# A 400 byte fill behind every second row gather in place of a 280 byte fill behind each one

## The chip, the cores and the metric

The kernel runs on one core of one Trainium2 chip. The metric is the device time of one execution in microseconds; the median of the runs shown counts.

## The reference, cut to what matters

The program is one layer of a graph network with attention, and behind it a mixture of experts. Only the first concerns the change, since it is there that rows are gathered.

```python
def _L0_gnn_ref(inputs, conv_weights, attn_l, attn_r, h_bias, edge_src, edge_dst, edge_type):
    # 3750 nodes, 123750 edges, 8 relations, 4 heads of 64
    feat_all = jnp.einsum('ni,rhid->rnhd', inputs, conv_weights)
    feat_src_e = feat_all[edge_type, edge_src]
    feat_dst_e = feat_all[edge_type, edge_dst]
    el = jnp.sum(feat_src_e * attn_l[edge_type], axis=-1)
    er = jnp.sum(feat_dst_e * attn_r[edge_type], axis=-1)
    e = jax.nn.leaky_relu(el + er, negative_slope=LEAKY_SLOPE)
    m = jax.ops.segment_max(e, edge_dst, num_segments=N_NODES)
    ex = jnp.exp(e - m[edge_dst])
    denom = jax.ops.segment_sum(ex, edge_dst, num_segments=N_NODES)
    alpha = ex / denom[edge_dst]
    h = jax.ops.segment_sum(alpha[..., None] * feat_src_e, edge_dst, num_segments=N_NODES)
    return h.reshape(N_NODES, OUT_FEAT) + h_bias
...
x = x + gnn(layernorm(x))
x = x + ffn(layernorm(x))      # 8 experts, 256 -> 512 -> 256, gelu, the two best of 8 by a gate
```

## The kernel before, in words

**First part** (to about 286 us). TensorE computes every node's features for every relation and ScalarE's queue writes them to `table` in HBM, one row of 264 floats for each node and relation. Beside it VectorE counts the edges of each node and ranks the nodes by degree; GpSimd gathers lists (`dchunk`, L337), scatters the nodes in their new order (`ranked`, L344) and gathers the first 64 indices of each node's edges (`idx_all`, L351, with a fill of its own behind each, L354, which the change leaves as it is).

**Second part.** The nodes are taken in W = 30 windows of 128, one node to a partition. For window w GpSimd issues one gather for each slot k: the instruction fetches, for each of the 128 nodes, the table row of its k-th incoming edge, into `rows[par][:, k, :]`. `par` is w mod 2, so there are two buffers of NS = 40 slots. The first SURE = 20 gathers of a window are always there; those after are issued one by one as long as the window's largest degree is over k (`more`). Edges past 40 come in batches of 8 into `xrows`, from L967 and L969 through the same helper (`gather`, L899) and without fills.

Behind each row gather stands a fill: `spaced_gather` (L922 to L925) issues the gather and then a memset of 280 bytes in each partition of a tile `spacer`, which nothing ever reads. The memsets at k = 9 and k = 19, and the one byte memset `space_end` at the end of a window, raise the semaphore `spaced`; GpSimd itself waits for it before it writes the same piece of `spacer` again.

**Order on GpSimd.** Between k = 7 and k = 8 of window w it issues the scatter of window w - 3's output (`scatter`, L907), which waits until VectorE has finished that output (L1228). At k = 0, 8, 16 and 24 it waits for `freed`: window w - 2 has folded that part of the buffer. The gathers of window w + 1 are issued while window w is worked on.

**The other engines.** When the rows of window w have landed (SyncE relays the last semaphore, L850), VectorE forms the attention scores (`prepare`, with L1023 the first instruction that needs the rows), ScalarE and VectorE weigh the rows (L1388, L1061), VectorE sums them (L1065), normalises the result and turns it into `z`; TensorE runs the experts of window w - 1 (L1485, L1499) and VectorE adds them up (L1222). In the first windows VectorE also works through the `xrows` batches (L1135 to L1142). After the last window its experts run alone.

Of the kernel before, what the change touches and what calls it, by code (L numbers as in the profile page):

```python
# [26 lines left out]
U8 = mybir.dt.uint8  # L27
AX_X = mybir.AxisListType.X

P = 128  # L30
# [69 lines left out]
def build(nc, x, src, dst, etype, conv, attn_l, attn_r, h_bias, gate_w, gate_b, W1, b1, W2, b2, out):  # L100
# [29 lines left out]
    with ctx:  # L130
        def sb(name, shape, dt=F32, stack=ctx):
            return stack.enter_context(nc.sbuf_tensor(name, shape, dt))


        ident = sb("ident", [P, P])
        idx_all = sb("idx_all", [P, W, CHUNK], U32)
        typ_all = sb("typ_all", [P, W, CHUNK], BF16)
        rank_sb = sb("rank_sb", [P, W, 4], I32)
        nb_row = sb("nb_row", [1, 2 * W], I32)
        slot_id = sb("slot_id", [P, CHUNK])  # L140
        wa = sb("wa", [P, KD, 2 * R * H])

        phase1(nc, sb, sem, locals())
        phase2(nc, sb, sem, locals())
# [483 lines left out]
def phase2(nc, sb, sem, env):  # L628
# [10 lines left out]
    SURE = 20  # L639
# [26 lines left out]
    oid = [sb(f"oid{i}", [P, 1], U32) for i in range(2)]  # L666
    typ_cur = [sb(f"typ_cur{i}", [P, CHUNK]) for i in range(2)]
    hot9 = sb("hot9", [P, NS, R1])
    PAUSE = 280
    spacer = sb("spacer", [P, SURE, PAUSE], U8)  # L670
    space_end = sb("space_end", [P, 1], U8)
    er_hot = sb("er_hot", [P, NS, H, R1])
    score = sb("score", [P, NS, H])
# [91 lines left out]
    def after(eng, s, value):  # L765

        if not isinstance(value, int) or value > 0:
            eng.wait_ge(s, value)

    def windows(eng, window):  # L770

        for w in range(2):
            window(w, w, 0)
        with eng.Fori(1, W // 2) as j:
            for par in range(2):
                window(j * 2 + par, par, j)
# [4 lines left out]
    def next_window(eng, act_on, w, par, half):  # L781

        if isinstance(w, int) or par == 0:
            act_on(w + 1, 1 - par, half + par)
        else:
            with eng.If(w < W - 1):
                act_on(within(w + 1), 1 - par, half + par)

    def alone(eng, passed):

        eng.sem_inc(passed, 1)
# [16 lines left out]
    def further_batches(eng, nb, batch, chunk):  # L808


        def chain(s, c, left):
            if s == SLOTS:
                return
            with eng.If(left > s):
                batch(s, c * SLOTS + s if not isinstance(c, int) else s, c)
                chain(s + 1, c, left)

        chain(STATIC, 0, nb)
        with eng.If(nb > SLOTS):
            with eng.Fori(1, (nb + (SLOTS - 1)) >> 3) as c:  # L820
                chunk(c)
                chain(0, c, nb - c * SLOTS)
# [67 lines left out]
    @block.gpsimd  # L890
    def _(pool):
        q = nc.gpsimd
        bt = Batches(pool, "pool")
        chunks = pool.alloc_register("pool_chunks")
        pool.reg_mov(chunks, 0)

        def gather(buf, landed, idx, slots, col=0):
            for k in slots:
                q.indirect_dma_start(buf[:, k, :], None, table,  # L899
                                     bass.IndirectOffsetOnAxis(idx[:, col + k:col + k + 1], 0)  # L900
                                     ).then_inc(landed, 16)

        def scatter(v, par, n=P):

            pool.wait_ge(out_ok, v + 1)
            alone(pool, pool_passed)
            q.indirect_dma_start(out, bass.IndirectOffsetOnAxis(oid[par][0:n, :], 0), xo[par][0:n, :],  # L907
                                 None).then_inc(out_done[par], 16)

        def static_rows(w, par, half):  # L910

            degree = pool.value_load(nb_row[0:1, bass.ds(w * 2 + 1, 1)], min_val=0, max_val=E)  # L912
            pool.wait_ge(idx_staged, w + 1)
            alone(pool, pool_passed)

            def freed_by(s):

                if not isinstance(w, int) or w >= 2:
                    pool.wait_ge(freed, (w - 2) * PAIRED + (s + 1))
                    alone(pool, pool_passed)  # L920

            def spaced_gather(k):  # L922

                gather(rows[par], row_landed[par][min(k // SLOTS, 2)], idx_st[par], (k,))
                return q.memset(spacer[:, k % SURE, :], 0)  # L925

            after(pool, spaced, w * 3)
            for k in range(SURE):
                if k == SLOTS and (not isinstance(w, int) or w >= 3):
                    scatter(w - 3, 1 - par)  # L930
                if k % SLOTS == 0:
                    freed_by(k // SLOTS)
                last = spaced_gather(k)
                if k in (SURE // 2 - 1, SURE - 1):
                    last.then_inc(spaced, 1)
            if isinstance(w, int):
                pool.wait_ge(cleared, 1)

            def more(k):

                if k < NS:
                    with pool.If(degree > k):  # L942
                        if k == 3 * SLOTS:
                            freed_by(3)
                        if k % (SURE // 2) == 0:
                            pool.wait_ge(spaced, w * 3 + k // (SURE // 2) - 1)
                            alone(pool, pool_passed)
                        spaced_gather(k)
                        more(k + 1)

            more(SURE)
            q.memset(space_end[:], 0).then_inc(spaced, 1)

        def window(w, par, half):

            next_window(pool, static_rows, w, par, half)
            nb, g = bt.enter(w)
            degree = pool.value_load(nb_row[0:1, bass.ds(w * 2 + 1, 1)], min_val=0, max_val=E)  # L958
            pool.wait_ge(xidx_staged, w + 1)
            alone(pool, pool_passed)  # L960

            def batch(s, i, c):

                pool.wait_ge(xfolded, g + (i - STATIC + 1))
                alone(pool, pool_passed)
                idx, lo = (idx_x[par], (s - STATIC) * SLOTS) if isinstance(c, int) else (xidx, s * SLOTS)
                gather(xrows, xrow_landed, idx, range(HALF), lo)  # L967
                with pool.If(degree > i * SLOTS + HALF):
                    gather(xrows, xrow_landed, idx, range(HALF, SLOTS), lo)  # L969

            def chunk(c):
                pool.reg_add(chunks, chunks, 1)
                n = pool.snap(chunks, min_val=1)
                pool.wait_ge(xblk_ok, n)
                alone(pool, pool_passed)
                q.indirect_dma_start(xidx[:], None, edge_row.rearrange("(n o) -> n o", o=1),
                                     bass.IndirectOffsetOnAxis(xblk[:], 0)).then_inc(xblk_in, 16)
                pool.wait_ge(xblk_in, n * 16)
                alone(pool, pool_passed)

            further_batches(pool, nb, batch, chunk)
            bt.leave(w, nb, g)

        static_rows(0, 0, 0)
        windows(pool, window)
        scatter(W - 3, 1)
        scatter(W - 2, 0)
        scatter(W - 1, 1, LAST)
        for i in range(2):
            pool.wait_ge(out_done[i], 16 * (W // 2))  # L990
# [583 lines left out]
```

## Time and profile before

| | |
|---|---|
| median of 3 runs | 1950.8 us (1950.03 to 1951.86) |
| profiled execution, own time | 1945.03 us |
| its span | 1943.3 us |
| mean granted TensorE clock | 0.822 |
| busy: POOL, PE, DVE, ACT | 1458.2, 1306.2, 1299.5, 788.2 us |
| row gathers, fills behind them | 982, 982 |

The time of an execution holds the span from the first to the last instruction and a little around it, here 1.7 us. The profiled execution is one run, and it lies 5.8 us below the median of the runs that were timed. A busy share is an average over parts of the program with different limits, so the chain of waits has to tell which engine counts.

### The profile page before, as it was taken

What the parts mean: (1) busy time and instruction counts of PE and PEld (TensorE: products, weight loads), DVE (VectorE), ACT (ScalarE), POOL (GpSimd) and SP (SyncE); (2) the same over time, 40 slices, a digit from 0 to 9 for tenths busy, and PEclk for the clock granted to TensorE, in tenths of its full rate; (3) what the DMA queues carried; (4) which work ended last, traced back from release to release, by engine and by line L of the source; (5) the groups of instructions that cost most, each with busy time, mean ns of one, the idle gap of its engine ahead of it and who ended that gap; (6) DMA issues with size and microseconds to landing.
All of it is one profiled execution on the core that took longest, in us unless ns stands there. A gap on an engine that the chain in (4) does not pass through costs nothing.

```text
span 1943.3 us, 29331 instructions
## 1 busy us (share of the span) xinstructions
PE 1306.2 (67%) x6897; PEld 1044.2 (54%) x6897; DVE 1299.5 (67%) x2572; ACT 788.2 (41%) x2841; POOL 1458.2 (75%) x2199
## 2 busy tenths in 40 slices
PE   4999950027584678585858586767768585857687
PEld 1444420026474667474747475656657474746575
DVE  4633012558786888686859595968687786868782
ACT  3544420215354444353435352534444453444441
POOL 0254568868888888888888888888888888888810
PEclk9999975559787888787878888787878697877888
DMA  6366768323333233333333333333333333333300
GB/s 155 111 204 171 197 177 256 98 76 95 85 93 98 83 93 94 93 93 93 95 92 94 93 95 92 94 90 96 95 93 95 93 94 92 95 93 95 89 17 4
DMA packets 86562, 202.20 MB, mean 104 GB/s; under 512 B 32445, under 2 KB 44663, under 8 KB 82341
## 3 DMA queue, kind: packets, MB, share of 16 engines
q0 software_dynamic: 57552, 147.97, 28.2%
q10 hardware_dynamic: 9596, 33.95, 5.8%
q1 hardware_dynamic: 19201, 18.44, 3.6%
q14 instruction: 201, 1.65, 0.3%
q8 instruction: 12, 0.20, 0.0%
HBM read 160.14 MB, written 40.07 MB: 103 GB/s over the span
## 4 chain that ended last, share of the span: by engine, by line
POOL 58%; issue 16%; DVE 4%; POOLq 4%; PE 2%; ACT 1%; DMA 1%; DVEq 0%; SPq 0%; ACTq 0%
POOL rows L899 40%; POOL spacer L925 16%; POOL out_dram L907 1%; PE y_ps L1499 1%; PE hid_ps L1485 1%; POOL xrows L899 1%; POOLq L942 1%; POOLq L912 1%; POOLq L958 1%; POOLq L802 1%; DVE fold_ps L1065 1%; DVE xo L1222 0%; DMA xrows<-table,idx_x 0%; ACT rows L1388 0%; DVE rows L1061 0%
## 5 line engine op out<-in xcount | busy, mean ns | idle before, releaser
L899 POOL DMA_INDIRECT rows<-table,idx_st x982 | 947.2, 965 | 212.3 <-issue 201.1
L1499 PE MATMUL y_ps<-w,hT 128*128 128x256 f32 (+1 forms) x1920 | 518.8, 427 | 353.9 <-ACT hT L1378 353.9
L1499 PEld LDWEIGHTS y_ps<-w,hT 128*128 128x128 f32 (+1 forms) x1920 | 392.5, 211 | 443.7 <-ACT hT L1378 378.6
L1485 PE MATMUL hid_ps<-zT,w 128*128 128x128 f32 (+1 forms) x3840 | 490.3, 290 | 0.0
L1485 PEld LDWEIGHTS hid_ps<-zT,w 128*128 128x128 f32 x3840 | 479.4, 206 | 13.8 <-issue 10.8
L1388 ACT ACTIVATE rows<-rows,ex 128x65 f32<-128x65 f32 x1320 | 326.1, 347 | 115.6 <-DVE ex L1052 115.6
L1378 ACT ACTIVATE hT<-hid_ps,b1t 128x128 f32<-128x128 f32 (+1 forms) x960 | 270.5, 364 | 209.3 <-PE hid_ps L1485 209.3
L1065 DVE TENSOR_TENSOR fold_ps<-rows,fold_ps 128x780 f32<-128x780 f32 (+1 forms) x348 | 326.5, 938 | 28.4 <-DVE rows L1061 5.0
L925 POOL MEMSET spacer<- 128x280 uint8 x982 | 342.2, 348 | 0.6
L579 PE MATMUL feat_ps<-wc,xnT 128*125 128x512 f32 x480 | 220.1, 603 | 0.5 <-ACT xnT L517 0.5
L1061 DVE TENSOR_TENSOR rows<-rows,fold_ps 128x2340 f32<-128x2340 f32 (+1 forms) x76 | 189.7, 2528 | 3.9 <-DVE rows L1061 3.9
L1222 DVE SCALAR_TENSOR_TENSOR xo<-y_ps,cw,xo 128x256 f32<-128x256 f32 (+1 forms) x240 | 115.6, 482 | 39.2 <-PE y_ps L1499 33.2
L579 PEld LDWEIGHTS feat_ps<-wc,xnT 128*125 128x125 f32 x480 | 86.5, 190 | 91.1 <-issue 91.1
L1344 ACT ACTIVATE th<-e_diff 128x160 f32<-128x160 f32 x30 | 10.1, 336 | 271.0 <-DVE e_diff L1041 271.0
L1023 DVE TENSOR_TENSOR score<-score,rows 128x160 f32<-128x160 f32 x30 | 9.8, 325 | 155.9 <-SPq L850 153.2
L532 ACT COPY stage<-feat_ps 125x512 f32<-125x512 f32 x120 | 69.7, 586 | 96.0 <-PE feat_ps L579 92.2
L337 POOL DMA_INDIRECT dchunk<-in_dst_dram,chunk_u x31 | 38.4, 1237 | 90.9 <-DVE chunk_u L417 81.7
L1458 PE MATMUL zt_ps<-ident,z 128*128 128x128 f32 x60 | 14.8, 335 | 135.1 <-DVE z L1169 135.1
L907 POOL DMA_INDIRECT out_dram<-xo,oid x30 | 30.1, 1004 | 91.8 <-DVE oid L1228 87.6
L1458 PEld LDWEIGHTS zt_ps<-ident,z 128*128 128x128 f32 x60 | 7.8, 174 | 137.0 <-DVE z L1169 136.9
L1469 PE MATMUL gate_ps<-ident,xnw 128*128 128x128 f32 x60 | 12.0, 283 | 87.6 <-ACT xnw L1355 87.6
L1366 ACT COPY zT<-zt_ps 128x256 f32<-128x256 f32 x30 | 11.2, 372 | 144.7 <-PE zt_ps L1458 144.7
(197 smaller groups left out, 1142.4 us busy)
## 6 DMA issues: line engine op xcount, KB each, us to landing
table<-stage ACTq DMA_DIRECT2D x30, 924.0 KB
rows<-table,idx_st POOLq DMA_INDIRECT x982, 2.8
w<-in_L_ffn_W_dram SPq DMA_DIRECT2D x16, 512.0 KB, 13.8
node_row<-ranked SPq DMA_DIRECT2D x30, 132.0 KB, 2.3
table<-stage ACTq DMA_DIRECT2D x30, 107.2 KB
x_all<-in_x_dram SPq DMA_DIRECT2D x2, 1120.0 KB
wc<-_L_gnn_conv_weights_dram ACTq DMA_DIRECT2D x2, 1024.0 KB, 9.4
x_all<-in_x_dram SPq DMA_DIRECT2D x2, 560.0 KB
```

The costliest lines, as they stand in the source:

```text
L532: a.copy(stage[i % NSTG][:, b * RB:(b + 1) * RB, 0:AGG].rearrange("p r (h c) -> p r h c", h=H)[:, :, :, 0:HD], feat_ps[b][0:TN, :].rearran ...
L579: last = m.matmul(feat_ps[b][0:TN, :], xnT[i % NXT][:, k, :], wc[:, k, b * BANK:(b + 1) * BANK], start=(k == 0), stop=(k == KD - 1))
L899: q.indirect_dma_start(buf[:, k, :], None, table, bass.IndirectOffsetOnAxis(idx[:, col + k:col + k + 1], 0)).then_inc(landed, 16)
L907: q.indirect_dma_start(out, bass.IndirectOffsetOnAxis(oid[par][0:n, :], 0), xo[par][0:n, :], None).then_inc(out_done[par], 16)
L925: return q.memset(spacer[:, k % SURE, :], 0)
L1061: return v.tensor_tensor(o, r, bc(ex_ps[:, :, lo:hi].rearrange("p h k -> p k h"), 3, HC), ALU.mult)
L1065: return v.tensor_tensor(lanes[:, 0:n], rows[par][:, lo:lo + n, 0:AGG], lanes[:, 0:n], ALU.add)
L1222: st.did(v.scalar_tensor_tensor(out=xo[par][0:n], in0=y_ps[p % 2][0:n, (e % 2) * D:(e % 2 + 1) * D], scalar=cw[0:n, e:e + 1], in1=xo[par][ ...
L1378: a.activation(hT[e % 2][:, m, 0:n], hid_ps[e % 2][:, m * P:m * P + n], ACT.Gelu, bias=b1t[:, e, m:m + 1]).then_inc(gelu_ok, 1)
L1388: last = a.activation(r, r, ACT.Copy, scale=ex[:, h, k:k + 1])
L1485: last = t.matmul(hid_ps[e % 2][:, m * P:m * P + n], w1[:, e, k, m * P:(m + 1) * P], zT[:, k, 0:n], start=(k == 0), stop=(k == KD - 1))
L1499: last = t.matmul(y_ps[p % 2][0:n, (e % 2) * D:(e % 2 + 1) * D], hT[e % 2][:, k, 0:n], w2[:, e, k, :], start=(k == 0), stop=(k == KH - 1))
```

## The change

The fill stands behind the odd gathers alone (k = 1, 3, 5, ...), and it is 400 bytes in place of 280. `spacer` has ten pieces in place of twenty.

```diff
-    PAUSE = 280
-    spacer = sb("spacer", [P, SURE, PAUSE], U8)
+    PAUSE = 400
+    spacer = sb("spacer", [P, SURE // 2, PAUSE], U8)
...
             def spaced_gather(k):
 
                 gather(rows[par], row_landed[par][min(k // SLOTS, 2)], idx_st[par], (k,))
-                return q.memset(spacer[:, k % SURE, :], 0)
+                if k % 2:
+                    return q.memset(spacer[:, k % SURE // 2, :], 0)
```

GpSimd's instructions at the start of a window, k = 0 to 3 (a row `DMA` is a gather, `spacer` the fill). Before:

```order
L899 DMA rows<-table,idx_st 128x264
L925 MEMSET spacer 128x280
L899 DMA rows<-table,idx_st 128x264
L925 MEMSET spacer 128x280
L899 DMA rows<-table,idx_st 128x264
L925 MEMSET spacer 128x280
L899 DMA rows<-table,idx_st 128x264
L925 MEMSET spacer 128x280
```

and with the change:

```order
L899 DMA rows<-table,idx_st 128x264 x2
L926 MEMSET spacer 128x400
L899 DMA rows<-table,idx_st 128x264 x2
L926 MEMSET spacer 128x400
L899 DMA rows<-table,idx_st 128x264 x2
```

Two gathers now follow each other with nothing between. In the part with branches, from k = 20 on, it reads so on GpSimd with the change:

```order
L943 COMPARE_AND_BRANCH
L899 DMA rows<-table,idx_st 128x264
L943 COMPARE_AND_BRANCH
L899 DMA rows<-table,idx_st 128x264
L926 MEMSET spacer 128x400
L943 COMPARE_AND_BRANCH
```

where before each gather had its fill and then its branch. Here a branch stands between the two gathers of a pair. A window whose number of gathers is odd ends on a gather without a fill behind it.

## Rows read from the trace of the kernel before

**Rows 1.** The page: busy time, and the chain that ended last, by engine and line.
```profile
PE 1306.2 (67%) x6897; PEld 1044.2 (54%) x6897; DVE 1299.5 (67%) x2572; ACT 788.2 (41%) x2841; POOL 1458.2 (75%) x2199
...
POOL 58%; issue 16%; DVE 4%; POOLq 4%; PE 2%; ACT 1%; DMA 1%; DVEq 0%; SPq 0%; ACTq 0%
POOL rows L899 40%; POOL spacer L925 16%; POOL out_dram L907 1%; PE y_ps L1499 1%; PE hid_ps L1485 1%; POOL xrows L899 1%; POOLq L942 1%; POOLq L912 1%; POOLq L958 1%; POOLq L802 1%; DVE fold_ps L1065 1%; DVE xo L1222 0%; DMA xrows<-table,idx_x 0%; ACT rows L1388 0%; DVE rows L1061 0%
```

**Rows 2.** Timeline, VectorE, first use of gathered rows (start, us, what [idle before <-releaser]).
```profile
515.79 0.19 DVE L1023 TENSOR_TENSOR score<-score,xrows 128x32 f32<-128x32 f32 x1 [7.42 <-SPq L850]
...
1001.95 0.33 DVE L1023 TENSOR_TENSOR score<-score,rows 128x160 f32<-128x160 f32 x1 [12.61 <-SPq L850]
...
1050.73 0.33 DVE L1023 TENSOR_TENSOR score<-score,rows 128x160 f32<-128x160 f32 x1 [0.23 <-DVE score L1020]
...
1818.73 0.33 DVE L1023 TENSOR_TENSOR score<-score,rows 128x160 f32<-128x160 f32 x1 [5.30 <-SPq L850]
...
1867.24 0.33 DVE L1023 TENSOR_TENSOR score<-score,rows 128x160 f32<-128x160 f32 x1 [0.23 <-DVE score L1020]
```

**Rows 3.** Timeline, GpSimd, first gathers of a window of 29 and of the next but one.
```profile
1002.43 1.03 POOL L899 DMA_INDIRECT rows<-table,idx_st  x1 [2.11 <-issue]
...
1104.58 1.08 POOL L899 DMA_INDIRECT rows<-table,idx_st  x1 [2.04 <-issue]
```

**Rows 4.** Timeline, GpSimd, the beat with fills: first and last of thirteen gathers.
```profile
1787.91 0.95 POOL L899 DMA_INDIRECT rows<-table,idx_st  x1 [0.17 <-issue]
...
1805.43 0.95 POOL L899 DMA_INDIRECT rows<-table,idx_st  x1 [0.17 <-issue]
```

**Rows 5.** Timeline, GpSimd, eight gathers without fills: first, second and last.
```profile
379.71 0.95 POOL L899 DMA_INDIRECT xrows<-table,idx_x  x1 [0.15 <-issue]
380.97 0.95 POOL L899 DMA_INDIRECT xrows<-table,idx_x  x1 [0.30 <-issue]
...
388.47 0.94 POOL L899 DMA_INDIRECT xrows<-table,idx_x  x1 [0.30 <-issue]
```

**Rows 6.** Groups by line, GpSimd, whole span (xcount | busy us, mean ns | idle before).
```profile
L899 POOL DMA_INDIRECT rows<-table,idx_st x982 | 947.2, 965 | 212.3 <-issue 201.1 <-POOL space_end L952 11.2
L925 POOL MEMSET spacer<- 128x280 uint8 x982 | 342.2, 348 | 0.6
L952 POOL MEMSET space_end<- 128x1 uint8 x30 | 3.5, 116 | 0.0
```

**Rows 7.** By line, fills and row gathers: duration ns min/median/max.
```profile
L925 POOL MEMSET spacer<- x982: 345/345/389, 286.9 to 1851.2; 128x280 uint8 x197
...
L899 POOL DMA_INDIRECT rows<-table,idx_st x982: 942/952/2679, 286.0 to 1850.2; - x197
```

**Rows 8.** Timeline, GpSimd, the end of a window.
```profile
1850.21 0.95 POOL L899 DMA_INDIRECT rows<-table,idx_st  x1 [0.16 <-issue]
...
1851.43 0.12 POOL L952 MEMSET space_end<- 128x1 uint8 x1
```

**Rows 9.** Groups by line, GpSimd, 286 us to 1818 us.
```profile
L899 POOL DMA_INDIRECT rows<-table,idx_st x961 | 927.2, 965 | 206.4 <-issue 195.2 <-POOL space_end L952 11.2
```

**Rows 10.** Timeline, GpSimd, the first of two scatters that wait.
```profile
532.30 1.01 POOL L907 DMA_INDIRECT out_dram<-xo,oid  x1 [4.27 <-DVE oid L1228]
```

**Rows 11.** Timeline, GpSimd and VectorE, a long gather and what ran beside it.
```profile
630.85 2.68 POOL L899 DMA_INDIRECT rows<-table,idx_st  x1 [0.17 <-issue]
...
630.38 2.33 DVE L1135 TENSOR_TENSOR xrows<-xrows,xex 128x2080 f32<-128x2080 f32 x1
632.74 0.43 DVE L1137 TENSOR_TENSOR acc<-acc,xex 128x260 f32<-128x260 f32 x1
```

**Rows 12.** Groups by line, GpSimd, list gathers without fills on 125 partitions.
```profile
L337 POOL DMA_INDIRECT dchunk<-in_dst_dram,chunk_u x31 | 38.4, 1237 | 90.9 <-DVE chunk_u L417 81.7 <-issue 9.1
```

**Rows 13.** DMA issues, median us to landing: 286 to 344 us, then 379 to 389 us.
```profile
rows<-table,idx_st POOLq DMA_INDIRECT x40, 6.1
...
xrows<-table,idx_x POOLq DMA_INDIRECT x8, 2.8
```

## The prediction

> **What bounds the kernel now.** I read the chain of waits first, since four engines are busy for 41% to 75% of the span and no share decides. The chain that ended last runs on GpSimd for 58% of the span, 40% in the row gathers and 16% in the fills behind them [rows 1]; its "issue" (16%) is for the most part the short idle pieces between a fill and the next gather. So the fill is not idle time somewhere: it stands in the chain.
>
> Next I looked at who waits for whom at the joint. VectorE's first use of a window's rows waited 12.61 us in the window at 1001.95 us and 0.23 us, for its own work, in the next [rows 2]. Over two windows VectorE loses 12.6 us to the gathers, and GpSimd idles between windows only for 0.3 to 0.9 us after one and about 2.1 us after the next [rows 3, 6]. GpSimd sets the pace, and VectorE has room to follow: a gain of up to 12.6 us in two windows would reach the end.
>
> Last the timeline of the beat itself. Twelve gathers with fills take 1787.91 to 1805.43, 17.52 us, or 1.460 us each: 0.95 gather, 0.345 fill, 0.165 idle [rows 4, 7]. The kernel also has gathers of the same table rows on the same 128 partitions without fills: eight of them start at 379.71 to 388.47, seven steps in 8.76 us, or 1.251 us each: 0.95 gather, 0.30 idle [rows 5]. A fill thus costs 0.209 us net, less than its own 0.345, because the idle time behind it is shorter than the one behind a bare gather.
>
> **The change, term by term.**
>
> 1. *Two steps of the beat.* Before, two gathers cost 2 x 1.460 = 2.920 us. Now the first is followed at once by the second, 1.251 us [rows 5]. The second has a fill of 400 bytes behind it.
>
> 2. *The larger fill.* No fill of 400 bytes is in the trace. One byte takes 116 ns and 280 bytes 345 ns (348 in the mean) [rows 6, 7]. That is (345 - 116) / 279 = 0.82 ns a byte, so 120 bytes more cost 0.099 us and the fill takes 0.444 us. The bounds: nothing more if the width does not count (it does, between 1 and 280), and 120/280 of 0.345 = 0.148 us if the whole of it grew in proportion. I take 0.099, since the line through both rows holds the fixed part as well. The second step is then 1.460 + 0.099 = 1.559 us.
>
> 3. *A pair* costs 1.251 + 1.559 = 2.810 in place of 2.920 us: **0.110 us gained a pair**. With the bounds of the fill it is 0.061 to 0.209.
>
> 4. *The branch* that now stands between two bare gathers from k = 20 on costs nothing: the burst of eight crosses such a branch in its middle and shows the same 0.30 us of idle time before each gather. GpSimd's sequencer works ahead while a gather of 0.95 us runs.
>
> 5. *Windows with an odd count.* Their last gather has no fill, and `space_end` follows it directly. Before, it began 0.27 us after the gather's end (a fill of 0.345 of which it overlaps the last 0.07) [rows 8]. I counted the gathers between successive `space_end` rows: 40, 24, 40, 25 in the first four windows, then 26 to 40, in twelve windows odd. Each odd one gains 0.27 us.
>
> 6. *How many count.* Of 982 gathers [rows 6], 961 start before 1818 us [rows 9]. The 21 of the last window are off the path: VectorE waits 5.30 us for the rows of the last window but one, at 1818.73, and for none at 1867.24 [rows 2]; between these it works through what it has, and the end, 1818.73 to 1943, is VectorE, ScalarE and TensorE. Two scatters, at 532.30 and, alike, at 644.55, wait 4.27 us each for VectorE's output [rows 10]; the eight gathers ahead of each only reach this wait earlier. That takes 16 off. The 29 windows to 1818 us have 475 pairs and 11 odd ends; less eight pairs, 467. Sum: 467 x 0.110 + 11 x 0.27 = 51.4 + 3.0 = **54.4 us**.
>
> 7. *What is late next.* Nothing new: in two windows with 29 and 37 gathers GpSimd gains 32 x 0.110 + 2 x 0.27 = 4.1 us of 102.15 [rows 3], and VectorE's wait falls from 12.6 to about 8.5. Before 700 us there are windows that VectorE sets for itself, but there too each stretch between two points at which GpSimd waits for VectorE holds a wait of VectorE for rows; the least is 7.42 us [rows 2], where that stretch (65 gathers) gains 3.6.
>
> **VectorE beside the gathers.** The gather at 630.85 took 2.68 us and not 0.95. VectorE was then in a multiply with both inputs in SBUF, from 630.38 to 632.71, and in a second one to 633.17 [rows 11]; two more gathers of 2.68 us stand beside the same pair of instructions. Others of 1.03 to 1.17 us lie beside shorter ones. All together this is 947.2 - 982 x 0.952 = 12.3 us [rows 6, 7]. A shift of GpSimd's beat changes which gather meets which instruction, not how many instructions VectorE has. So I put the change at nothing, with 12 us more or 12 us less as the bounds (twice as much, or none).
>
> The Trainium skill, SBUF — State Buffer, "Who interferes with whom", says that VectorE and GpSimd share one pair of ports, that whoever comes first holds it for its whole instruction, and that a VectorE instruction with two SBUF inputs stands against GpSimd instructions that read SBUF. This trace agrees (2.68 us against 0.95 us). By that rule a fill, which only writes, would hold off VectorE's two-port instructions as a gather does, and fewer fills would give VectorE some time back; it waits for GpSimd anyway, so the sum would stay.
>
> **Against its own time.** The profiled execution took 1945.03 us; with the change it would take 1890.6. It lies 5.8 us below the median of the runs, 1950.8; I take the same gain off the median: **1896.4 us**.
>
> **The rivals.**
>
> *A bare second gather is dearer than the burst shows* (slower). In the list gathers without fills thirty in a row take 1.21 us each: 38.4 us for 31, less 2.04 for the first, cold one [rows 12]. If the second gather of each pair took 1.21 in place of 0.95 us, 467 x 0.26 = 121 us would come on top: 1896.4 + 121 = 2018 us. It decides from 54.4 / 467 = 0.12 us a pair on. Against it: those gathers write 125 partitions, not 128, and read another table, while 24 bare gathers of just these rows took 0.95 each. For it: the longest run of bare row gathers is sixteen with a break in it, and the new beat must hold for 1500 us. A backlog that builds up slowly and then stalls the descriptors would be the same rival. 12 in 100 for all prices on this side.
>
> The Trainium skill, DMA: Bandwidth & Descriptors, "Anatomy of one DMA", says that many descriptors can be issued before their incremental cost shows. No run of nine gathers would show such a cost by that rule; a steady beat could. It leaves the numbers above as they are.
>
> *Something paces the gathers at 1.46 us in the long run* (no change): GpSimd writes faster and is held back by as much, and the time stays 1950.8. Against it: in the first window, beside the loads of the weights, the gathers took 6.1 us to land and not 2.8 [rows 13], so about four were under way at once, and the beat stayed 1.46; and the burst at 1.25 us landed in the same 2.8. 6 in 100.
>
> *Half the gain* from more collisions with VectorE, or a fill at its upper bound: 54.4 - 12.3 = 42 us, 1909 us; both together (467 x 0.049 = 23 us less again), 19 us, 1932. 6 in 100.
>
> *VectorE becomes the bound:* it would need a gain over 12.6 us in two windows; this is 4.1. I give it nothing.
>
> **How the numbers follow.** The forecast has 76 in 100, with its own range of 1889 to 1903: 2 us for the fill's slope, 5 us for collisions and for the difference between a profiled and a timed run. The range given goes to 1928, so that most of the half gains are in it; what is left out is no change, slower, and a rest, some 20 in 100. The lower end is 1887. A measurement of this kernel can tell about 0.2%, 4 us, from no change. Faster takes the forecast and the half gains, 0.82; the same 0.05; slower 0.13.
>
> **What would show it.** About 485 fills of 0.44 us; gathers in pairs 1.25 us apart, then 1.56; gathers still 0.95 us; 98.1 us in place of 102.15 from a long window's end over the next two; VectorE's wait for rows near 8.5 us; time to landing still 2.8 us; the last window's VectorE part as it was, 54 us earlier. It is wrong if second gathers read well over 0.95, if the idle time between the gathers of a pair is over 0.41 us, if the landing time climbs along a window, or if GpSimd has a new wait for `freed`.

## The result, and the profile after

The changed kernel takes 1885.99 us (median of 4 runs, 1882.78 to 1888.87), the kernel before in the same measurement 1951.33 us (4 runs, 1950.03 to 1958.03). The ratio is 0.9658, with a 95% interval of 0.9629 to 0.9687: faster by 65.3 us, or 3.4%. The forecast was 1896.4 us, a gain of 54.4. The sign and the reading of what bounds the kernel came as forecast; the gain is 11 us larger, and the time lies 1 us below the range's lower end, because a gain of 15 us between the windows was not in the sum.

The profiled execution took 1888.87 us with a span of 1887.1. Its page, the busy times and then the chain that ended last by engine and by line (before: [rows 1]):

```profile
PE 1310.8 (69%) x6897; PEld 1046.0 (55%) x6897; DVE 1286.1 (68%) x2572; ACT 787.4 (42%) x2841; POOL 1332.8 (71%) x1702
...
POOL 47%; issue 18%; DVE 7%; PE 6%; POOLq 3%; ACT 2%; DMA 1%; DVEq 0%; SPq 0%; ACTq 0%
```

GpSimd has 497 instructions less and is busy for 125.4 us less. The chain still runs on it.

The timeline of GpSimd after, at the first gather of a window of 29, at three gathers inside that window, at the first gather of the next window but one, and at the last gather of all with `space_end` behind it (start, us, what [idle before <-releaser]; before: [rows 3, 4, 8]):

```profile
980.06 0.95 POOL L899 DMA_INDIRECT rows<-table,idx_st  x1 [0.94 <-POOL space_end L953]
...
1001.12 0.95 POOL L899 DMA_INDIRECT rows<-table,idx_st  x1 [0.17 <-issue]
1002.37 0.95 POOL L899 DMA_INDIRECT rows<-table,idx_st  x1 [0.31 <-issue]
1003.32 0.45 POOL L926 MEMSET spacer<- 128x400 uint8 x1
1003.93 0.95 POOL L899 DMA_INDIRECT rows<-table,idx_st  x1 [0.16 <-issue]
...
1077.49 0.94 POOL L899 DMA_INDIRECT rows<-table,idx_st  x1 [0.94 <-POOL space_end L953]
...
1787.93 0.95 POOL L899 DMA_INDIRECT rows<-table,idx_st  x1 [0.17 <-issue]
1788.88 0.12 POOL L953 MEMSET space_end<- 128x1 uint8 x1
```

A pair goes from 1001.12 to 1003.93: 2.81 us, 1.25 to the bare gather and 1.56 over the fill. At the end of a window with an odd count `space_end` now begins where the gather ends, 0.27 us earlier than in [rows 8]. From the first gather of one window of 29 to that of the next but one it is 97.43 us, against 102.15 before [rows 3]. What the prediction does not have is the idle time ahead of these first gathers: 0.94 us, where it was 2.11 and 2.04 [rows 3].

The timeline of VectorE after, its first use of the rows in the same windows and in the last window but one (before: [rows 2]):

```profile
980.62 0.33 DVE L1024 TENSOR_TENSOR score<-score,rows 128x160 f32<-128x160 f32 x1 [9.14 <-SPq L850]
...
1028.20 0.33 DVE L1024 TENSOR_TENSOR score<-score,rows 128x160 f32<-128x160 f32 x1 [0.23 <-DVE score L1021]
...
1078.42 0.33 DVE L1024 TENSOR_TENSOR score<-score,rows 128x160 f32<-128x160 f32 x1 [8.40 <-SPq L850]
...
1759.38 0.33 DVE L1024 TENSOR_TENSOR score<-score,rows 128x160 f32<-128x160 f32 x1 [3.83 <-SPq L850]
```

VectorE waits 9.14 and 8.40 us where it waited 12.61 and 12.58, and is still the one that waits.

The three parts of the span, before and then after: to the first row gather, from there to the first gather of the last window, and the rest (stretch, us, then busy time of TensorE, its weight loads, VectorE, ScalarE and GpSimd, then TensorE's granted clock, the share of the DMA engines and GB/s):

```profile
0.00:286.00 286.00, 246.38 (x687) 116.46 (x687) 99.72 (x277) 117.77 (x256) 117.07 (x152) 0.98 0.61 168
286.00:1819.70 1533.70, 973.11 (x5690) 856.02 (x5690) 1125.56 (x2149) 622.64 (x2395) 1309.75 (x2002) 0.79 0.36 98
1819.70:1943.30 123.60, 86.73 (x520) 71.67 (x520) 74.19 (x148) 47.75 (x190) 31.39 (x47) 0.85 0.12 27
```

```profile
0.00:292.50 292.50, 249.62 (x687) 117.70 (x687) 99.67 (x277) 117.37 (x256) 117.10 (x151) 0.97 0.60 164
292.50:1758.40 1465.90, 966.87 (x5664) 851.12 (x5665) 1111.40 (x2146) 622.31 (x2395) 1187.05 (x1515) 0.81 0.37 103
1758.40:1887.00 128.60, 94.35 (x549) 77.15 (x547) 75.06 (x150) 47.73 (x190) 28.64 (x36) 0.85 0.12 27
```

The middle, where the change works, is 67.8 us shorter. The first part is 6.5 us longer in this execution and the last 5.0. So the two profiled executions differ by 56.2 us of span, near the forecast, while the middle differs by more and two other parts take some of it back. The section on the prediction takes these apart.

### The profile page after: what moved, and what is told of

It is laid out like the page before. It is cut to its first block, busy times and chain, and to the rows that moved or that the text cites. A ratio compares the mean times of both kernels' runs of the same rounds, so it can differ in the third digit from the quotient of the medians.

```text
span 1887.1 us, 28834 instructions
## 1 busy us (share of the span) xinstructions
PE 1310.8 (69%) x6897; PEld 1046.0 (55%) x6897; DVE 1286.1 (68%) x2572; ACT 787.4 (42%) x2841; POOL 1332.8 (71%) x1702
## 4 chain that ended last, share of the span: by engine, by line
POOL 47%; issue 18%; DVE 7%; PE 6%; POOLq 3%; ACT 2%; DMA 1%; DVEq 0%; SPq 0%; ACTq 0%
POOL rows L899 36%; POOL spacer L926 9%; PE y_ps L1500 3%; PE hid_ps L1486 3%; POOL out_dram L907 1%; ACT rows L1389 1%; DVE rows L1062 1%; DVE fold_ps L1066 1%; POOL xrows L899 1%; POOLq L912 1%; POOLq L943 1%; POOLq L959 1%; DMA xrows<-table,idx_x 1%; POOLq L802 1%; DVE xrows L1136 0%
## 5 line engine op out<-in xcount | busy, mean ns | idle before, releaser
L899 POOL DMA_INDIRECT rows<-table,idx_st x982 | 944.2, 961 | 271.4 <-issue 247.4
L926 POOL MEMSET spacer<- 128x400 uint8 x485 | 218.7, 451 | 0.2
L1367 ACT COPY zT<-zt_ps 128x256 f32<-128x256 f32 x30 | 11.2, 372 | 147.8 <-PE zt_ps L1459 147.8
```

Of the source, the lines that this page charges most:

```text
L899: q.indirect_dma_start(buf[:, k, :], None, table, bass.IndirectOffsetOnAxis(idx[:, col + k:col + k + 1], 0)).then_inc(landed, 16)
L926: return q.memset(spacer[:, k % SURE // 2, :], 0)
```

## The experiments

**What they had to tell apart.** The first theory is the prediction's with one thing added: GpSimd's chain of gathers, fills and short idle pieces sets the pace, the fills are pure cost in it, and the gain over 54.4 us comes from the place where GpSimd's program goes round its loop over the windows (L774), once in two windows. This place is called the joint below; there the idle time before the first gather fell from 2.1 to 0.94 us. The rival to the first half is that the gathers are paced by something else and need the fills. For the joint there are two theories. *Lead*: GpSimd's sequencer, the part that reads the instructions and hands them to the engine (rows marked POOLq), comes to the jump earlier, since the last instructions of a window are fewer or take longer. *Size*: the loop holds less code. Every kernel here computes the full result. The kernel before took 1947.7 us (7 runs) beside the first four, 1949.61 (11 runs) beside the next four, 1947.95 (7 runs) beside the last.

### No fills: e1_no_fill

```diff
-                return q.memset(spacer[:, k % SURE, :], 0)
+                if k in (SURE // 2 - 1, SURE - 1):
+                    return q.memset(spacer[:, k % SURE, 0:1], 0)
```

> No fill behind the row gathers but one byte at k = 9 and k = 19. If nothing paces the gathers, the beat is 1.25 us, GpSimd needs about 87 us for two windows and VectorE, which needed 89.4 of its own in the changed kernel (97.8 less its wait of 8.4), becomes the bound: GpSimd waits for freed buffers, VectorE no longer waits for rows, two windows take about 89.5 us in place of 102.15, and the time falls to about 1775 to 1800 us. If a long row of gathers is held at some pace (the reason a fill would be there), gathers grow well over 0.95 us or their landing over 2.8 us, and the time stays at or above the changed kernel's 1886.

Measured: 1773.86 us, ratio 0.9102 (0.9079 to 0.9125). Row gathers by line (duration ns min/median/max, first and last start), and the chain that ended last:

```profile
L899 POOL DMA_INDIRECT rows<-table,idx_st x982: 940/946/3094, 285.1 to 1646.3; - x197
```

```profile
DVE 37%; PE 22%; issue 9%; ACT 9%; POOL 4%; DVEq 2%; DMA 0%; POOLq 0%; ACTq 0%; SPq 0%
```

982 gathers run at a median of 0.946 us over 1361 us with hardly a fill (60 of one byte), and their time to landing has the same median of 2.8 us, with 3.6 us at the most. This ends the rival of a dearer second gather (1.21 us) and that of a pace of 1.46 us. The chain has moved: GpSimd holds 4% of it, VectorE 37%. The timeline of VectorE in e1_no_fill, three windows in a row:

```profile
882.30 0.33 DVE L1024 TENSOR_TENSOR score<-score,rows 128x160 f32<-128x160 f32 x1 [0.23 <-DVE score L1021]
922.88 0.33 DVE L1024 TENSOR_TENSOR score<-score,rows 128x160 f32<-128x160 f32 x1 [0.23 <-DVE score L1021]
971.09 0.32 DVE L1024 TENSOR_TENSOR score<-score,rows 128x160 f32<-128x160 f32 x1 [0.23 <-DVE score L1021]
```

It doesn't wait for rows in these windows (the last wait for rows is at 397 us), and two windows take 88.8 us: 102.15 less its former wait of 12.6 is 89.5. So [rows 2] gave the whole room that there was, and VectorE bounds once it is used up.

### One byte behind every gather: e2_one_byte

```diff
-                return q.memset(spacer[:, k % SURE, :], 0)
+                return q.memset(spacer[:, k % SURE, 0:1], 0)
```

> One byte behind every gather. By the net price of a fill (its own time less 0.136 us of idle time that it replaces) this beat is 0.952 + 0.116 + 0.165 = 1.233 us, slightly shorter than without fills, and the time is that of no fills within 5 us, since VectorE sets it. If what a fill does is to separate two gathers, this kernel differs from the one without fills: it would be faster than that by much.

Measured: 1780.44 us, ratio 0.914 (0.9114 to 0.9165). It is 6.6 us above e1_no_fill, a little over what was expected. The late start of its row gathers (292.0 us in its profile, 285.1 there) doesn't account for it alone: from the first row gather to VectorE's first use of the rows of the last window but one it takes 1358.0 us, against 1352.3 in e1_no_fill. Where these 5.7 us come from is not shown. Beyond them it doesn't matter that something stands between two gathers, only how long it takes. But the first gather behind the loop's joint waits longer than in any other kernel. The timeline of GpSimd in e2_one_byte:

```profile
928.96 0.94 POOL L899 DMA_INDIRECT rows<-table,idx_st  x1 [3.03 <-issue]
929.91 0.12 POOL L925 MEMSET spacer<- 128x1 uint8 x1
930.21 0.95 POOL L899 DMA_INDIRECT rows<-table,idx_st  x1 [0.19 <-issue]
```

### The change's beat without its pairs: e3_each_210

```diff
-    PAUSE = 280
+    PAUSE = 210
```

> 210 bytes behind every gather: the same mean pace as the changed kernel (2 x 1.405 = 2.81 us for two gathers) without pairs. If only the pace counts, the time is that of the changed kernel, about 1886. If the changed kernel's shorter gap at the loop's end comes from its fewer instructions (the sequencer reaches the branch earlier, or the loop is shorter), that gap is here as before, 2.05 us or somewhat more (2.3 if the lead is eight instructions), thirteen times, and the odd windows lack their 0.27 us: about 1886 + 15 + 3 = 1904.

Measured: 1894.17 us, ratio 0.9724 (0.9698 to 0.975). The fill takes 0.290 us, so a gather costs 0.952 + 0.290 + 0.16 = 1.40 us, which is half a pair of the change. The idle time at the loop's joint stays, 1.9 to 2.6 us at thirteen places, 2.20 in the mean. From the first row gather to the first of the last window it takes 1479.4 us (284.25 to 1763.69), the change 1465.9: nearly the same beat is 13.5 us dearer without the shorter joint and the odd ends, where 18 were expected. The total is 10 us under what was expected. Part of it may be the start: the row gathers began at 284.3 us here and at 292.5 in the change's first profile, and that start scatters, as shown below. This is the run that parts the two gains: a beat of 1.40 us gives some 54 us (1947.7 less 1894.2), the rest of the change's gain is in the joints and the odd ends.

### Bare gathers only late, or only early, in a window: e4_pairs_from_24 and e5_pairs_to_24

```diff
-                return q.memset(spacer[:, k % SURE, :], 0)
+                if k < 24 or k % 2:
+                    return q.memset(spacer[:, k % SURE, :], 0)
```

> The kernel before, with the fill of even gathers left out from k = 24 on. Two theories of the gap at the loop's end (2.05 us before, 0.93 with the change). Lead: GpSimd's sequencer runs a fixed number of instructions ahead of the engine, fewer instructions in the last 10 us before the branch mean an earlier branch, so the gap falls to 0.93 as in the changed kernel though only 2 to 8 fills a window are gone. Size: the loop body is shorter; with some 30 fewer instructions and not 150 the gap stays near 2 us.

Measured (one run): 1910.29 us, with 844 fills of 280 bytes. The idle time at the joint is 0.94 us, as lead would have it: 138 fills less are enough. The middle, from the first row gather to the first of the last window, shows the price of the joint beside that of the fills. It takes 1489.5 us, 44.2 less than before, and 138 x 0.209 = 28.8 us for the fills with 15.2 at the joints make 44.0. The second kernel has the condition the other way round:

```diff
-                return q.memset(spacer[:, k % SURE, :], 0)
+                if k >= 24 or k % 2:
+                    return q.memset(spacer[:, k % SURE, :], 0)
```

> The mirror of the last run: fills of 280 bytes, left out behind even gathers below k = 24 and kept behind each from k = 24 on. It drops more fills (twelve a window) than that run did, but none near the end of a long window. Lead: the gap at the loop's end is back at about 2.05 us. Size of the loop body: it is 0.93 us, since this body is shorter than that of the last run. The time by the sum: 28 windows x 12 x 0.209 = 70 us below before, about 1878.

Measured (one run): 1872.39 us, where 1878 were expected without a gain at the joint, with 623 fills; the idle time at the joint is 0.94 us here too. In this kernel the end of a window is as before, a fill behind every gather, and the joint is short all the same. So lead alone falls, and this run sides with size as the last one sided with lead: neither theory holds as it was put.

### The pairs with the old fill: e6_second_280

```diff
-    PAUSE = 400
+    PAUSE = 280
```

> The changed kernel with fills of 280 in place of 400 bytes: the other half of the change alone. A pair costs 1.251 + 1.460 = 2.711 us. By the sum with the measured fill of 0.450 us for 400 bytes it is 467 x 0.105 = 49 us below the changed kernel's 1886: about 1837, gap at the loop's end 0.93. VectorE's wait for rows falls from 8.4 to about 5 us in two windows. If the larger fill were what makes the pair safe, gathers or their landing would get longer and the time would not be below 1886.

Measured: 1834.22 us, ratio 0.943 (0.9394 to 0.9466). The diff is against the changed kernel, so the larger fill alone costs 48.7 us beside e8_change_again below (1882.88). 485 fills at 451 ns in place of 351 are 48.5 us: nothing of the larger fill is hidden. The time is near what was expected (1837), the gathers take 962 ns in the mean as in the change (961), and their time to landing keeps its median of 2.8 us, so it is not the larger fill that makes the pairs possible. The groups by line of GpSimd in e6_second_280:

```profile
L899 POOL DMA_INDIRECT rows<-table,idx_st x982 | 944.3, 962 | 268.6 <-issue 245.3 <-POOL space_end L953 23.2
L926 POOL MEMSET spacer<- 128x280 uint8 x485 | 170.5, 351 | 0.1
```

### Also no fills in the lists' loop: e7_no_fill_lists

```diff
-                g.memset(spacer[:, w, :], 0)
```

> No fills behind the row gathers (one byte at k = 9 and 19) and none behind the list gathers of the first part either (L354). Those 30 fills cost 30 x 0.209 = 6.3 us on GpSimd. If the list gathers are on the path of the first part, the second part starts up to 6 us earlier and the time is 1768; if TensorE and the writes of the table set it, nothing changes: 1774.

This is e1_no_fill with the fill of L354 taken out too, before the first row gather. Measured: 1771.66 us, ratio 0.91 (0.9074 to 0.9126), no different from e1_no_fill. The row gathers begin at 285.1 and 285.2 us: those fills lie beside a wait for other work.

### The change once more: e8_change_again

> The changed kernel once more, to see what of its 65 us belongs to the middle and what to the first part, whose instructions it does not touch. The middle (first row gather to the first one of the last window) should read 1465.9 us again, within 3 us; the first part 284 to 293 us, as its start came at 285.98 and 292.53 us in the two profiles so far. If the change moved the first part, it would read 292.5 again and no profile of a kernel with another fill would lie near it.

Measured: 1882.88 us (6 runs), ratio 0.9662 (0.9638 to 0.9686). The row gathers begin at 284.42 us and the last window's at 1750.42: a middle of 1466.0 us, against 1465.9 in the first profile of the change. The middle repeats to 0.1 us, while the first part differs by 8 us between two executions of the same kernel.

### More code, the same work: e9_dead_code

```diff
+    tiny = sb("tiny", [P, SURE + 1], U8)
...
+                if k == NS:
+                    with pool.If(degree > 4096):
+                        for i in range(21):
+                            q.memset(tiny[:, i:i + 1], 0)
                 if k < NS:
```

> The changed kernel with 21 one byte fills added at the end of each copy of the row gathers behind a branch that is never taken: nothing more is executed than a compare at k = 40, but GpSimd's loop is about as long as before the change. In the runs so far all kernels whose instruction queue moved 201 packets have a gap of 2.1 to 3.0 us at the loop's end and all with 187 or 186 packets have 0.93, the fourteen packets being one for each pass of the loop. If the length of the code is the cause, this kernel moves about 201 packets again and its gap is 2 us or more, 13 times 1.1 us or more: about 1884 + 15 = 1899. If the executed fills are the cause (how far the sequencer is ahead of the engine), it stays at 187 packets or at least at a gap of 0.93 and at 1884.

The last four lines stand in `more`, in the changed kernel, and the branch is never taken. Measured: 1882.94 us, ratio 0.9667 (0.9639 to 0.9694), with 201 packets in the instruction queue, as before, in place of the change's 187, and with 0.93 us of idle time at the joint. The amount of code alone doesn't lengthen it, so size falls too.

**The joint itself.** The way of GpSimd's sequencer around it can be followed in three of its own instructions: the last load of a window's count (L958, in the change L959), the branch of the loop (L774), and the first load at the loop's start (L912). By line, in the kernel before (count, duration ns, start us):

```profile
L958 POOLq TENSOR_LOAD <-nb_row x1: 286/286/286, 993.4 to 993.4; - x1
...
L774 POOLq COMPARE_BRANCH  x1: 45/45/45, 997.1 to 997.1; - x1
...
L912 POOLq TENSOR_LOAD <-nb_row x1: 297/297/297, 1000.7 to 1000.7; - x1
```

and in the kernel after:

```profile
L959 POOLq TENSOR_LOAD <-nb_row x1: 285/285/285, 969.7 to 969.7; - x1
...
L774 POOLq COMPARE_BRANCH  x1: 45/45/45, 971.1 to 971.1; - x1
...
L912 POOLq TENSOR_LOAD <-nb_row x1: 289/289/289, 974.5 to 974.5; - x1
```

From the branch to the loop's first load it takes much the same in both, 3.6 and 3.4 us. From the load to the branch it takes 3.7 us before and 1.4 after. The DMA queues say what stands in those 2.3 us. Before, 993.4 to 997.1 us:

```profile
q0 software_dynamic: 138, 0.38, 37.0%
q14 instruction: 1, 0.01, 0.5%
```

and after, 969.7 to 971.1 us:

```profile
DMA packets 53, 0.16 MB, mean 112 GB/s; under 512 B 16, under 2 KB 16, under 8 KB 53
...
q0 software_dynamic: 53, 0.16, 41.8%
```

A packet of the instruction queue falls between load and branch before, at 995.5 us, and none after, where one comes at 968.4, ahead of the load, and the next at 971.8, behind the branch. It is the same in e3_each_210 (a packet at 970.0, load 968.0, branch 971.6) and e2_one_byte (922.0, between 920.3 and 923.6), and there is none between the two at this joint in e4_pairs_from_24 and e5_pairs_to_24. In the kernels before and after two packets fall between the branch and the loop's start.

The other joints of the traces bear this out, thirteen a kernel. In the kernel before, e2_one_byte and e3_each_210 a packet starts 1.7 to 2.4 us behind the load at each of the 39 joints, and from load to branch it takes 3.3 to 4.0 us. In the other eight kernels it takes 1.4 us at all 104. Now and then a packet falls between the two there as well, but within 1.3 us of the load (0.6 in e9_dead_code at this joint), and nothing waits. In e9_dead_code, where the amount of code is back, one packet stands 0.4 to 1.0 us ahead of the load at each joint and not behind it. So what counts seems to be where in the code the packet is due, and not how much code there is; no run put the old place back on purpose. The queue's rows don't say for which engine a packet is.

All this lies ahead of the engine: while the sequencer goes this way, GpSimd still works off the last gathers and fills. What counts is which is done first. The chain of waits of the kernel before at the joint:

```profile
999.93 0.35 POOL spacer L925
1000.28 0.04 POOL space_end L952
...
1000.68 0.30 POOLq L912
...
1001.51 0.06 POOLq L919
...
1001.63 0.80 issue
1002.43 1.03 POOL rows L899
```

and of the kernel after:

```profile
978.63 0.45 POOL spacer L926
979.08 0.05 POOL space_end L953
979.13 0.02 issue
979.15 0.06 POOLq L919
...
979.27 0.79 issue
980.06 0.95 POOL rows L899
```

After, the sequencer has reached the start of the loop at 974.5 us and stands there, ready, when `space_end` ends. Before, `space_end` began at 1000.21 and the sequencer was still to run through L912 to L919. The way of the sequencer is from the last load to its first instruction behind the branch (at 1000.5 us before, at 974.3 after, 0.2 us ahead of the load in the rows above); its lead is from that last load to the start of `space_end`. For the joint of each kernel that lies between 900 and 1000 us:

| kernel | way, us | lead, us | idle before the first gather, us |
|---|---|---|---|
| before | 7.1 | 6.8 | 2.1 |
| e3_each_210 | 6.8 | 6.4 | 2.2 |
| e2_one_byte | 6.7 | 5.5 | 3.0 |
| after | 4.6 | 9.3 | 0.94 |
| e9_dead_code | 4.6 | 9.3 | 0.93 |
| e5_pairs_to_24 | 4.3 | 6.8 | 0.94 |
| e4_pairs_from_24 | 4.5 | 8.9 | 0.94 |
| e1_no_fill | 4.9 | 13.0 | 0.93 |

Where the lead is over the way by 2.5 us and more, 0.93 us are left. In the first three rows the way is the longer one, and the idle time is 1.8 us plus what the way has over the lead, within 0.1 us at all 39 joints of these kernels: a lead shorter by 1 us costs 1 us. Between e5_pairs_to_24 and before the lead is equal (6.8) and only the way differs: the shorter way alone is enough. Whether the longer lead alone would be was not tried.

## Why the prediction came out as it did

**Held.** Step 1, the bare second gather: 1.25 us, and 0.95 for the gather itself. Step 3, a pair at 2.810 us: 2.81. Step 4, the branch at nothing: the idle time between the gathers of a pair is 0.305 us in the mean over all 485 pairs, branches between them or not. Step 5, the odd ends: `space_end` directly behind the gather. Step 7, nothing new late: 97.43 us for two windows (98.1 forecast), VectorE's wait 9.1 and 8.4 us (8.5), and the scatter at 532 us waits 4.87 where it waited 4.27 [rows 10]. The reading of the bound held in full: GpSimd paces, VectorE follows, and e1_no_fill shows where that ends.

**Step 2, mis-sized by a little.** The fill takes 450 ns, not 444 (busy time of both groups, kernel after):

```profile
L899 POOL DMA_INDIRECT rows<-table,idx_st x982 | 944.2, 961 | 271.4 <-issue 247.4 <-POOL space_end L953 23.2 <-DVEq L1086 0.6
L926 POOL MEMSET spacer<- 128x400 uint8 x485 | 218.7, 451 | 0.2
```

That is 467 x 0.006 = 2.8 us less gain. With 1, 210, 280 and 400 bytes at 0.12, 0.290, 0.345 and 0.450 us the line through two points was right to 2%.

**Beside the gathers.** Long gathers by VectorE's multiplies were put at nothing; L899's busy time went from 947.2 [rows 6] to 944.2 us. The bounds were 12 us either way; 3 came, on the good side. VectorE in turn was busy for 13.4 us less (1299.5 to 1286.1), in the direction of the prediction's remark on the ports; what made it so was not tested, and it was waiting anyway.

**The step that failed** stands at the start of the prediction, under what bounds the kernel, where GpSimd's idle time between windows is "0.3 to 0.9 us after one and about 2.1 us after the next". It was read as a fixed price of the joint and so has no term in step 6. Over its thirteen places it was 27.4 us before and 12.2 after: 15.2 us gained, nowhere in the sum. The wait at the joint was put at nothing gained, without a reason. The sum becomes 54.4 - 2.8 + 15.2 = 66.8 us, against 67.8 in the middle, of which the last joint's 1.6 us (2.57 to 0.95) lie off the path, and 66.7 between the medians of e8_change_again and the kernel before beside it. The prediction had the word for the cause in its step 4, that the sequencer works ahead while a gather runs, but did not ask where it doesn't get far enough ahead. The rows had the question in them: 2.11 and 2.04 us behind one joint [rows 3], and 0.93 behind the other (11.2 us over twelve [rows 6]), with the same instructions of the engine at both.

**Why the profiled pair shows only 56.2 us.** From VectorE's first use of the rows of the last window but one to the end it is 124.6 us before and 127.7 after. TensorE's clock was granted at 0.72 for one stretch of 6.0 us there before, and at 0.68 for three stretches after (windows of the kernel before and then of the kernel after, columns as above):

```profile
1910.00:1916.00 6.00, 6.00 (x24) 3.08 (x24) 0.12 (x1) 0.84 (x4) 0.00 (x0) 0.72 0.01 3
```

```profile
1839.50:1844.60 5.10, 5.10 (x34) 4.95 (x33) 2.62 (x15) 1.35 (x6) 0.98 (x1) 0.68 0.08 27
1844.80:1850.00 5.20, 5.20 (x18) 2.29 (x17) 0.00 (x0) 0.78 (x5) 0.00 (x0) 0.68 0.00 0
1861.60:1866.90 5.30, 5.30 (x18) 2.35 (x17) 0.00 (x0) 0.84 (x4) 0.00 (x0) 0.68 0.00 0
```

As an estimate, taken at the full clock these 15.6 us would be 10.6, the 6.0 us before 4.3, so the clock makes some 5.0 less 1.7, or 3.3 us, about the 3.1 that are found. (The last part counted from the last window's first gather grew by 5.0, since that gather, with the shorter joint, is earlier against VectorE's work.) But nothing ties this to the pairs: the same stretch takes 127.4 to 129.7 us in all ten other profiles, 127.8 in e8_change_again and 129.6 in e3_each_210, which has no pairs. It is the one profile of the kernel before that is short, an execution that took 1945.03 us where the median is 1950.8. Why the clock fell less there is open. That the gain of the profiled pair lies near the forecast of 54.4 is chance. The 6.5 us in the first part don't come with the change either. From 220 to 230 us the clock stood at 0.66, behind a stretch in which TensorE had been busy for only 6.75 of 10 us; before, it was busy throughout and at 1.00. The start of the row gathers scatters from 284.3 to 292.5 us over the eleven profiles of this study, though the instructions up to there are the same in all but e7_no_fill_lists, and is 284.42 in the second profile of the change. In the four that start at 290.6 us or later (after, e2_one_byte, e5_pairs_to_24, e9_dead_code) TensorE paused for 3.3 to 4.3 us between 200 and 230 us and the clock then fell, and in none of the others.

**The rivals.** The dearer second gather (12 in 100) and the pace of 1.46 us (6) fell with e1_no_fill. Half a gain (6) did not come. VectorE as the bound was rightly given nothing for this change, and becomes true once all fills go. The unknown that did matter was not among them: the rivals all asked what could take gain away, and none what the fills could be costing elsewhere. The lower end of the range, 1887, left 9 us for everything of this kind, where 15 came.

**What a packet may stand for.** At the joint the runs show packets of the instruction queue, one less in a pass now: 13 in most passes of 102 us over two windows before, 12 in most of those of 97 us after. The Trainium skill, Advanced Engine Details and Errata, "ISA Cache", says that a sequencer keeps its code in no more than two lines of 256 instructions each, configurable. The runs agree as far as they go: with half the fills out of the loop's code a pass takes one packet less, and with the never taken branch of e9_dead_code it takes 13 again. The Trainium skill gives such a line there as 16 KB, while the queue moved 201 packets in 1.65 MB before, 8.2 KB each; that a packet is a line is not shown. It gives no time for a missing line in that section; that the 2.3 us are the wait for code is inferred from the packet's place.

**The best version measured.** Without fills the kernel takes 1772 to 1774 us, 9% under the kernel before and 6% under the change. The fills bought nothing here that any run could show.

## What to carry to other kernels

An instruction that is there only to keep others apart is a claim about the queue behind them; measure the time to landing and the duration of the neighbours with and without it; where both stay the same, as here, nothing is left that it buys in time. Price such an edit by the whole step of the beat, idle time included, and not by the duration of the instruction: a fill of 0.345 us cost 0.209 here. And before an idle time marked "issue" is taken as fixed, look at the sequencer's own rows around it: where the program jumps back, what decides is whether the sequencer's lead over its engine is longer than its way round, and cheaper instructions shorten that lead (5.5 us with fills of one byte, 6.8 with 280).

## What the runs showed of the hardware

- A jump back to the start of GpSimd's window loop costs its sequencer 2.9 to 3.7 us from the branch to the next instruction, with two or three packets of the instruction queue in between, at all thirteen joints of the eleven profiles. It costs the engine nothing beyond 0.93 us where the sequencer is ahead by 6.8 us or more and the way is 4.3 to 4.9 us.
- Where the way from the last load to the loop's start is longer than the lead, the idle time is 1.8 us plus the difference (before, e2_one_byte, e3_each_210). So instructions that are cheaper for the engine can lengthen an idle time: one byte fills in place of 280 byte ones made the joint's 2.1 us into 3.0.
- A fill on GpSimd takes about 0.12 us plus 0.82 ns for each byte of a partition, from 1 to 400. Behind a fill the next gather starts after 0.165 us, behind a bare gather after 0.30: behind a fill of one byte 0.19, so that such a fill is free in the beat (1.25 us with it and without).
- 982 indirect gathers of 128 rows over 1361 us, 1.25 us apart within a window, land in the same median of 2.8 us as with 1.46 us steps (before and e1_no_fill).
